# Grouped attention, new turn table: angles and weight splits move, two shifts per unit go to GpSimd, the maximum comes last in its turn

## The chip, the cores and the metric

The kernel runs on one core of a Trainium2 chip. The metric is the device time of one execution in microseconds. The core's engines have queues of their own and meet at semaphores: the tensor engine (PE; PEld is its weight load), the vector engine (DVE), the scalar engine (ACT), GpSimd (POOL) and SyncE (SP), which issues the large transfers.

## The reference

Four layers, each a cross-attention and a feed-forward part, on 4 x 256 tokens of width 256 with a context of 1601 rows. The change touches the attentions of layers 1 and 3, which have 16 query heads of width 128 over 4 key/value heads. Cut to what matters:

```python
# layer 3 (layer 1 has the same form, with x normalised first)
q = rms_norm((x @ Wq).reshape(B, S, 16, 128), q_norm_w)
k = rms_norm((ctx @ Wk).reshape(B, S_ctx, 4, 128), k_norm_w)
v = (ctx @ Wv).reshape(B, S_ctx, 4, 128)
probs = softmax(einsum("bqhd,bkhd->bhqk", q, repeat(k, 4)) * 128 ** -0.5)
out = einsum("bhqk,bkhd->bqhd", probs, repeat(v, 4)).reshape(B, S, 2048) @ Wo
# layer 1 only: the 256 tokens are keys too, and q and k are turned by position
emb = concat(pos * inv_freq, pos * inv_freq)          # 64 frequencies
x = x * cos(emb) + rotate_half(x) * sin(emb)
```

## The kernel before, in words

`run_layers` runs the stages one after another. `grouped_attention` is called twice: as `a1` with `rope=True` (layer 1, the rope stage) and as `a3` with `rope=False` (layer 3, the last attention stage). Each call has a first block (`plan_first`), which prepares the first group, and a main block with all the attention.

The main block works through 16 groups, a batch and a key/value head each. A group has two units of 512 query columns, and a unit one turn per tile of 128 keys: KT = 15 tiles in the rope stage (13 of context, 2 of tokens) and 13 in the last. So a group has 30 or 26 turns. In turn n the tensor engine makes `scores(n)` (L1184 to L1186) and `values(n - KT - 6)` (L1196). The scalar engine makes `exp(n - KT - 5)` (L1332) and `keep(n)`, a scaled copy of the scores into a ring (L1317). The vector engine makes `highest(n)`, the running maximum over a unit (L1551). The shift by the maximum, `shift(n - KT - 3)`, is made in the ring by the vector engine (L1568) or by GpSimd (L1438); `by_vector` says which, from the tile's number.

When a unit is through, MX transposes the running maximum on the tensor engine (L1152) and reduces it on the vector engine (L1559). NB broadcasts it on the tensor engine (L1163) and copies it on the scalar engine (L1326). MX0 and NB0 stand in turns 16 and 17 of a rope group (14 and 15 of the other), MX1 and NB1 in turns 1 and 2. In the vector engine's queue MX comes first in its turn, ahead of `highest` and `shift`. NB's matmuls wait for the reduce and, since they overwrite what the shifts read, for the vector engine's last shift of the unit before.

All other work is in a table written out by hand, `GROUP_TURNS`: a string for each turn, whose tasks prepare the next group. Every engine walks it in order. The names: KV, Q are products with their copies and squares (L1084, L1098; L1276, L1280, L1291; L1518, L1523); KN, QN norms; KR, QR rotation on GpSimd in two items each, products (L1393, L1394) and sums (L1400, L1401); KX, QX, OX transposes (L1113, L1122, L1130) with a high and a low part (L1489); Y the output product (L1141); N, NZ, NX the normalised tokens; PR, PX the positions; RA the angles on the vector engine and RS their sines on the scalar engine (L1339); GP, GA gathers from the stage before, in group 0 only (L1446, L1498). A `<` means the task of the group before. RA, RS and the other tasks of `NEXT_BATCH` are only done once per batch: the early ones in the third group of a batch, the `late` ones in the fourth, for the first three batches. The products and transposes share two banks of PSUM in turn.

W is the weights: W0 for K and V, W1 for Q, W2 for the output product. Each weight is used as a high and a low half. For the first groups (W0 and W1: groups 0 and 1; W2: groups 0 to 3) W splits them: SP loads them into the one buffer `wf`, the scalar engine copies the high half (L1260), the vector engine subtracts (L1476), and SP stores both halves and then issues the next load (L980). Later groups fetch the halves (L993). So SP's order is

```python
i = splits[("W", g, k)]
sp.wait_ge(w_lo, i)
store_weights(g, k)
if i < len(weights):
    load_weights(*weights[i][1:])
```

## Time and profile before

| | |
|---|---|
| median of 3 runs | 3602.94 us (3602.02 to 3603.24) |
| profiled execution, its own time | 3602.94 us |
| its span, first to last instruction | 3601.2 us |
| busy: PE, DVE, ACT, POOL | 3316.4, 2280.7, 2246.0, 1559.2 us |
| mean granted clock of the tensor engine | 0.959 |
| rope stage, main block | from 544 us to 1717 us |
| last attention stage, main block | from 2487 us to 3477 us |

A row of the profile names an engine, a line of the kernel, an operation and its tiles (output, then inputs, buffer numbers left out). A wait is idle time of an engine ahead of an instruction, put down to the instruction that released it. The granted clock is 1.00 at 2.4 GHz and 0.50 at 1.2 GHz; a stretch in between holds both.

### The profile page before, as it was taken

To read this page: it belongs to the slowest core of one execution; us is meant where nothing else is said; L and a number is where in the kernel's file an instruction comes from. 1 tells how busy PE (TensorE), PEld (TensorE's weight loads), DVE (VectorE), ACT (ScalarE), POOL (GpSimd) and SP (SyncE) were. 2 spreads that over 40 slices of the span, in tenths; PEclk is the share of its full clock that TensorE was granted. 3 is DMA by queue.
4 is the path that set the end of the run, shared out by engine and by line. 5 is a ranking of instruction groups with operands and counts; after the bars stand their busy time and mean duration, and the time that the engine had idled before them with its cause. 6 is when DMAs were issued, how large, how long until landed. Compare 5 with 4: busy or idle time off the path is not lost. (4 is left out here: it accounts for less than half of the span.)

```text
span 3601.2 us, 64159 instructions
## 1 busy us (share of the span) xinstructions
PE 3316.4 (92%) x23332; PEld 2857.9 (79%) x23332; DVE 2280.7 (63%) x4533; ACT 2246.0 (62%) x5204; POOL 1559.2 (43%) x1584
## 2 busy tenths in 40 slices
PE   6859958999999999999799999888999999999999
PEld 5658957888889888888666666577899999999888
DVE  8976746766676676666777777535655555555544
ACT  3326736777777767776376676515777777777743
POOL 0012146766667665763220220112565555555534
PEclk8879978999999999999899999989999999999999
DMA  5216522110120021000200000113221111120011
GB/s 189 92 40 218 216 89 85 68 61 30 48 79 30 30 84 42 31 19 24 92 19 38 1 38 1 75 39 115 71 84 48 54 73 42 43 84 31 30 39 39
DMA packets 74457, 227.83 MB, mean 63 GB/s; under 512 B 7780, under 2 KB 29472, under 8 KB 69152
## 3 DMA queue, kind: packets, MB, share of 16 engines
q1 hardware_dynamic: 68288, 184.34, 14.4%
q0 software_dynamic: 3696, 37.68, 2.8%
q8 instruction: 188, 3.08, 0.4%
q10 hardware_dynamic: 2160, 1.71, 0.2%
q14 instruction: 125, 1.02, 0.1%
HBM read 178.60 MB, written 45.11 MB: 62 GB/s over the span
## 5 line engine op out<-in xcount | busy, mean ns | idle before, releaser
L1551 DVE SCALAR_TENSOR_TENSOR a_peak<-ps,a_k_rstd,a_peak 128x512 f32<-128x512 f32 (+1 forms) x768 | 575.9, 750 | 617.6 <-ACT a_ring L1317 612.1
L1196 PE MATMUL ps<-a_v_rows,a_ring 128*128 128x129 f32 (+1 forms) x7168 | 934.8, 275 | 7.6 <-DVE a_o_rows L1577 3.8
L1317 ACT ACTIVATE a_ring<-ps,a_k_rstd 128x512 f32<-128x512 f32 (+1 forms) x896 | 615.5, 688 | 496.5 <-PE ps L1186 456.7
L1196 PEld LDWEIGHTS ps<-a_v_rows,a_ring 128*128 128x128 f32 (+1 forms) x7168 | 877.8, 191 | 26.0 <-ACT a_ring L1332 9.2
L1438 POOL TENSOR_TENSOR a_ring<-a_ring,a_negb 128x512 f32<-128x512 f32 (+1 forms) x506 | 645.7, 1297 | 246.0 <-ACT a_negb L1326 236.8
L1332 ACT ACTIVATE a_ring<-a_ring 128x512 f32<-128x512 f32 (+1 forms) x896 | 562.7, 631 | 18.6 <-DVE a_ring L1568 13.4
L1184 PE MATMUL ps<-a_qt,a_kt 128*128 128x512 f32 (+1 forms) x896 | 423.5, 473 | 5.0 <-PEq L73 5.0
L1084 PE MATMUL ps<-a_wr,a_ct 128*128 128x256 f32 (+1 forms) x2496 | 382.4, 291 | 36.8 <-DMA a_ct<-ctx_lo 15.9
L1084 PEld LDWEIGHTS ps<-a_wr,a_ct 128*128 128x128 f32 (+1 forms) x2496 | 346.6, 190 | 83.4 <-DVE a_k_rows L1518 25.6
L1186 PE MATMUL ps<-a_qt,a_kt 128*128 128x512 f32 (+1 forms) x896 | 356.6, 398 | 0.0
L1185 PE MATMUL ps<-a_qt,a_kt 128*128 128x512 f32 (+1 forms) x896 | 355.4, 397 | 0.0
L3407 ACT ACTIVATE a_probs<-ps 128x1024 f32<-128x1024 f32 x224 | 229.5, 1024 | 136.1 <-PE ps L3261 135.3
L1568 DVE TENSOR_TENSOR a_ring<-a_ring,ps 128x512 f32<-128x512 f32 x390 | 262.6, 676 | 2.8 <-ACT a_negb L1326 2.8
L3599 DVE TENSOR_REDUCE a_parts<-ps 128x1 f32<-128x448 f32 x384 | 222.1, 618 | 57.4 <-PE ps L3223 52.1
L1186 PEld LDWEIGHTS ps<-a_qt,a_kt 128*128 128x128 f32 (+1 forms) x896 | 166.8, 186 | 43.0
L1373 POOL TENSOR_SCALAR a_k_sq<-a_k_sq 128x4 f32<-128x4 f32 (+2 forms) x128 | 28.5, 223 | 368.7 <-ACT a_v_rows L1280 362.4
L1184 PEld LDWEIGHTS ps<-a_qt,a_kt 128*128 128x128 f32 (+1 forms) x896 | 169.9, 190 | 8.2 <-issue 5.6
L1185 PEld LDWEIGHTS ps<-a_qt,a_kt 128*128 128x128 f32 (+1 forms) x896 | 169.9, 190 | 2.5
L3261 PE MATMUL ps<-a_qt,a_kt 128*128 128x512 f32 x448 | 164.2, 448 | 2.5 <-ACT a_qt L3394 2.3
L1276 ACT ACTIVATE a_square<-ps 128x128 f32<-128x128 f32 (+1 forms) x448 | 124.6, 278 | 62.7 <-PE ps L1084 57.4
L1518 DVE TENSOR_TENSOR a_k_rows<-ps,a_kw 128x128 f32<-128x128 f32 (+1 forms) x448 | 126.2, 283 | 53.3 <-ACT a_v_rows L1280 53.2
L3223 PE MATMUL ps<-a_kt,a_qt 128*128 128x448 f32 (+1 forms) x512 | 154.3, 368 | 4.9 <-ACT a_kt L3375 1.2
(465 smaller groups left out, 6016.5 us busy)
## 6 DMA issues: line engine op xcount, KB each, us to landing
a_wr<-a_w SPq DMA_DIRECT2D x96, 512.0 KB, 4.5
a_w<-a_wr SPq DMA_DIRECT2D x32, 512.0 KB, 3.9
a_wr<-a_w SPq DMA_DIRECT2D x48, 256.0 KB, 3.5
a_ct<-ctx_hi SPq DMA_DIRECT2D x8, 1090.0 KB, 5.7
a_ct<-ctx_lo SPq DMA_DIRECT2D x8, 1090.0 KB, 7.9
f_we<-in_f_experts SPq DMA_DIRECT2D x8, 1088.0 KB, 8.5
...
```

The costliest lines, as they stand in the source:

```text
L1084: ins = pe.matmul(out[0:r, 0:2 * HD], src, wr[0][v][:, c * 2 * HD:(c + 1) * 2 * HD], start=(n == 0), stop=(n == 3 * DC - 1))
L1184: pe.matmul(out, kt[0][:, at:at + r], qt[0][:, cols], start=True, stop=False)
L1185: pe.matmul(out, kt[0][:, at:at + r], qt[1][:, cols], start=False, stop=False)
L1186: pe.matmul(out, kt[1][:, at:at + r], qt[0][:, cols], start=False, stop=True).then_inc(st_ready, 1)
L1196: ins = pe.matmul(m.ps[:, 6 + i // 2, (i % 2) * 256:(i % 2) * 256 + VW], slot(n)[0:r, i * P:(i + 1) * P], v_rows[u // NG % 2][0:r, t, :], ...
L1317: act.activation(slot(n)[0:r, :], m.ps[0:r, SCORE_BANKS[n % 3], :], ACT.Copy, scale=k_rstd[0:r, g % 2, t:t + 1]).then_inc(kept, 1)
L1332: act.activation(slot(n)[0:r, :], slot(n)[0:r, :], ACT.Exp).then_inc(exp_done, 1)
L1438: pool.tensor_tensor(slot(n)[0:r, :], slot(n)[0:r, :], negb[0:r, u % 2, :], ALU.add)\
L1551: dve.scalar_tensor_tensor(out=peak[0:r, :], in0=m.ps[0:r, SCORE_BANKS[n % 3], :], scalar=k_rstd[0:r, u // NG % 2, t:t + 1], in1=(slot(n - ...
L1568: dve.tensor_tensor(slot(n)[0:r, :], slot(n)[0:r, :], m.ps[0:r, MAX_BANK, :], ALU.add)\
L3407: act.activation(flat2(probs[n % 3][:, :, :]), flat2(m.ps[:, first:first + 2, :]), ACT.Exp)\
L3599: dve.tensor_reduce(to, slot(("R", h, j))[:, 0:n], AX.X, ALU.max, negate=True).then_inc(neg_done, 1)
```

## The change

`GROUP_TURNS` gets new tables. In the rope stage the angles go from RA0 to RA8 in one group, with RS in the next, to RA0 to RA2 in the third group of a batch and RA3 to RA9 and RS0 in the fourth; the query rotations QR move from turns 9 to 12 to turns 12 to 15, the key rotations KR0 to KR3 from 14, 15, 17, 18 to 16 to 19, KR4 and KR5 by two turns and one or two; KX1 goes from 22 to 23 and KX2 from 27 to 29; QN, N, NZ move by a few turns. W0 goes from turn 4 of the next group to turn 29 (25 in the other stage) of its own, right behind W2, which in the last stage goes from 25 to 24; W1 goes from 12 to 8.

The angles are computed into the tables themselves: the sine's and the cosine's argument each get a tensor, the cosine's by adding a quarter turn and taking a whole turn off where it is over half a turn, and RS makes both sines in place. That is 11 vector operations for 9. The wait for the last rotation of the batch before, which RS had, is now RA3's. `by_vector` gives the vector engine every second tile of the rope stage (7 of 15) where it had 9 of 15 (tiles 1, 2, 3, 5, 6, 7, 9, 10, 11). MX on the vector engine moves into the turn's task list, behind `outputs`, `highest` and `shift`.

```diff
--- before.py
+++ after.py
@@ -715,22 +715,22 @@
 
 GROUP_TURNS = {
     True: (
-        "QX1<", "MX1 KR6<", "NB1 KR7<", "Q0", "W0< PR0 GP4", "RS0 GP5", "Q1 GA4 GP6", "KX3< PX0 GA5 GP7 QN0",
-        "KV0 QN1 GA6 GP8", "OX0 KV1 QR0 RA0 GA7 GP9", "KV2 QR1 RA1 GA8 GP10", "KV3 QR2 RA2 GA9 GP11",
-        "KV4 KN0 QR3 W1 RA3 GA10 GP12", "KV5 RA4 GA11 GP13", "KV6 KR0 RA5 GA12 GP14", "KV7 KR1 RA6 GA13 GP15",
-        "MX0 KN1 GA14", "NB0 KV8 KR2 GA15", "QX0 KR3 RA7", "KV9 RA8", "KX0 KV10 N0", "KV11", "KX1 KN2 KV12",
-        "OX1 KR4 NZ0", "Y0 KR5", "KV13", "Y1", "KX2 KV14", "W2", "KN3 NX0",
+        "QX1<", "MX1 KR6<", "NB1 KR7<", "Q0 RA3", "RA4 PR0 GP4", "RA5 GP5", "Q1 RA6 GA4 GP6",
+        "KX3< RA7 PX0 GA5 GP7", "KV0 QN0 W1 RA8 GA6 GP8", "OX0 KV1 RA9 GA7 GP9", "KV2 QN1 RS0 RA0 GA8 GP10", "KV3 GA9 GP11",
+        "KV4 KN0 QR0 RA1 GA10 GP12", "KV5 QR1 GA11 GP13", "KV6 QR2 RA2 GA12 GP14", "KV7 QR3 GA13 GP15",
+        "MX0 KN1 KR0 GA14", "NB0 KV8 KR1 GA15", "QX0 KR2", "KV9 KR3", "KX0 KV10", "KV11 N0", "KV12",
+        "OX1 KX1 KN2", "Y0 NZ0", "KV13 KR4", "Y1 KR5", "KV14", "W2", "KX2 W0 KN3 NX0",
     ),
     False: (
-        "QX1<", "MX1", "NB1 KX2< KN3<", "Q0", "KX3< W0<", "", "Q1", "QN0", "OX0 KV0", "KV1 QN1", "KV2", "KV3 N0",
-        "KV4 KN0 W1", "KV5 QX0", "MX0 KV6 NZ0", "NB0", "KV7", "KX0 KV8", "KN1", "KV9", "KV10", "OX1 KX1", "Y0",
-        "KV11 KN2", "Y1", "KV12 W2 NX0",
+        "QX1<", "MX1", "NB1 KX2< KN3<", "Q0", "KX3<", "", "Q1", "QN0", "OX0 KV0 W1", "KV1 QN1", "KV2", "KV3 N0", "KV4 KN0",
+        "KV5 QX0", "MX0 KV6 NZ0", "NB0", "KV7", "KX0 KV8", "KN1", "KV9", "KV10", "OX1 KX1", "Y0",
+        "KV11 KN2", "Y1 W2", "KV12 W0 NX0",
     ),
 }
 
 FIRST_TASKS = {
     True: (
-        "GP0 V0 GP1 PR0 GP2 PX0 RA0 RA1 RA2 RA3 GA0 RA4 GA1 RA5 RA6 GA2 RA7 GP3 KV0 GA3 RA8 KV1 KV2 N0 KV3 "
+        "GP0 V0 GP1 PR0 GP2 PX0 RA0 RA1 RA2 RA3 GA0 RA4 GA1 RA5 RA6 GA2 RA7 GP3 KV0 GA3 RA8 RA9 KV1 KV2 N0 KV3 "
         "RS0 KN0 KV4 NZ0 KV5 V1 NX0 KR0 KV6 KV7 QN0 QN1 KR1 Q0 Q1 KX0 W1 KV8 KV9 KV10 KN1 QR0 QR1 KV11 KN2 QR2 "
         "KV12 KN3 QR3 KV13 KR2 KV14 KR3 QX0 KR4 KR5 KR6 KR7 KX1 KX2 KX3 QX1 W0"
     ),
@@ -757,7 +757,7 @@
     if kind in ("GP", "GA"):
         return g == 0
     if kind in NEXT_BATCH:
-        late = kind == "RS"
+        late = kind == "RS" or kind == "RA" and i >= 3
         return g % KVH == (KVH - 1 if late else KVH - 2) and g + KVH < GROUPS
     if kind in ("MX", "NB"):
         return g > 0 if i else g < GROUPS
@@ -873,7 +873,7 @@
             u, t = divmod(n, KT)
             if u == UNITS - 1:
                 return t % 3 > 0
-            return t % 4 > 0 and t < KT - 2 if rope else t % 4 == 3
+            return t % 2 == 1 if rope else t % 4 == 3
 
         by_turn = [by_vector(n) for n in range(TURNS)]
         shifts = {v: list(itertools.accumulate(int(b == v) for b in by_turn)) for v in (False, True)}
@@ -1332,11 +1332,9 @@
                         act.activation(slot(n)[0:r, :], slot(n)[0:r, :], ACT.Exp).then_inc(exp_done, 1)
 
                     def RS(g, _i):
-                        if attend:
-                            act.wait_ge(k_ready, rotated_k[("KR", g - 1, 2 * len(KB) - 1)])
-                        for i, (angle, table) in enumerate(((ang, cs[:, 1, :, :]), (tmp, cs[:, 0, :, :]))):
+                        for i in range(2):
                             act.wait_ge(angles, 2 * (turn_of_batch(g) - 1) + i + 1)
-                            act.activation(table, angle, ACT.Sin).then_inc(tab_ok, 1)
+                            act.activation(cs[:, i, :, :], cs[:, i, :, :], ACT.Sin).then_inc(tab_ok, 1)
 
                     def end_high(k):
                         act.wait_ge(end_turned, k + 1)
@@ -1595,14 +1593,15 @@
 
                     def RA(g, i):
 
+                        if i == 3 and attend:
+                            dve.wait_ge(k_ready, rotated_k[("KR", g - 1, 2 * len(KB) - 1)])
                         c1 = 6.28125
                         c2 = float(np.float32(0.0019353071795864769))
                         c3 = 2 * np.pi - c1 - c2
                         magic = 12582912.0
                         PI = 3.1415925
+                        cos, sin = cs[:, 0, :, :], cs[:, 1, :, :]
                         if i == 0:
-                            if turn_of_batch(g) > 1:
-                                dve.wait_ge(tab_ok, 2 * (turn_of_batch(g) - 1))
                             step(dve.tensor_tensor(ang, pos_f[:, :].unsqueeze(2).to_broadcast([P, KT, half]),
                                                    invf[:, :].unsqueeze(1).to_broadcast([P, KT, half]), ALU.mult))
                         if i == 1:
@@ -1610,16 +1609,17 @@
                         if i == 2:
                             step(dve.tensor_scalar(tmp, tmp, -magic, None, ALU.add))
                         if i in (3, 4, 5):
-                            step(dve.scalar_tensor_tensor(out=ang, in0=tmp, scalar=-(c1, c2, c3)[i - 3],
-                                                          in1=ang, op0=ALU.mult, op1=ALU.add))
+                            step(dve.scalar_tensor_tensor(out=sin, in0=tmp, scalar=-(c1, c2, c3)[i - 3],
+                                                          in1=ang if i == 3 else sin, op0=ALU.mult, op1=ALU.add))
                         if i == 6:
-                            dve.tensor_scalar(ang, ang, PI, -PI, ALU.min, ALU.max).then_inc(angles, 1)
+                            step(dve.tensor_scalar(cos, sin, np.pi / 2, None, ALU.add))
                         if i == 7:
-                            dve.wait_ge(angles, 2 * (turn_of_batch(g) - 1) + 1)
-                            step(dve.scalar_tensor_tensor(out=tmp, in0=ang, scalar=-1.0, in1=ang,
-                                                          op0=ALU.mult, op1=ALU.min))
+                            step(dve.tensor_scalar(tmp, cos, np.pi, -2 * np.pi, ALU.is_gt, ALU.mult))
                         if i == 8:
-                            dve.tensor_scalar(tmp, tmp, np.pi / 2, None, ALU.add).then_inc(angles, 1)
+                            step(dve.tensor_tensor(cos, cos, tmp, ALU.add))
+                        if i == 9:
+                            dve.tensor_scalar(cos, cos, PI, -PI, ALU.min, ALU.max).then_inc(angles, 1)
+                            dve.tensor_scalar(sin, sin, PI, -PI, ALU.min, ALU.max).then_inc(angles, 1)
 
                     def end_low(k):
                         dve.wait_ge(end_hi, k + 1)
@@ -1630,11 +1630,9 @@
                         dve.wait_ge(zeroed, ZEROED)
                         dve.wait_ge(norm_in, 16 * NORMS)
                     does = {"GA": GA, "PR": PR, "PX": PX, "RA": RA, "W": W, "N": N, "NZ": NZ, "NX": NX, "KV": KV, "Q": Q,
-                            "KX": KX, "QX": QX, "OX": OX, "Y": Y}
+                            "KX": KX, "QX": QX, "OX": OX, "Y": Y, "MX": MX}
                     for n, turn in enumerate(turns):
                         v, s = n - VALUE_LAG, n - SHIFT_LAG
-                        for _task, g, i in (task for task in turn if task[0] == "MX"):
-                            MX(g, i)
                         if attend and 0 < v < TURNS and v % KT == 0:
                             outputs(v // KT - 1)
                         if attend and n < TURNS and n % KT:
```

## Rows read from the trace of the kernel before

**Rows 1.** Windows: busy time (instructions) of PE, PEld, DVE, ACT, POOL; PEclk, DMA share, GB/s.

```profile
1201.97:1273.27 71.30, 70.10 (x506) 63.68 (x505) 44.35 (x79) 50.83 (x132) 46.66 (x50) 1.00 0.11 38
...
1273.27:1349.87 76.60, 71.65 (x511) 64.08 (x510) 57.81 (x98) 51.37 (x133) 53.51 (x51) 1.00 0.22 78
...
2858.50:2920.50 62.00, 61.47 (x449) 56.45 (x448) 35.71 (x70) 44.95 (x118) 33.79 (x35) 1.00 0.29 103
```

**Rows 2.** The tensor engine's waits, 544 to 1640: us in total, times, longest us.

```profile
PE ps L1084 <- DVE a_k_rows L1518: 15.5, 21, 2.0
...
PE ps L1141 <- DVE a_ot L1489: 11.5, 14, 0.8
...
PE ps L1163 <- DVE a_negmax L1559: 3.3, 4, 1.1
```

**Rows 3.** Order of time, all engines, one maximum of the rope stage: start, duration, instruction.

```profile
801.06 0.60 PE L1152 MATMUL ps<-ident,a_peak 128*128 128x128 f32 x4
...
801.26 0.69 ACT L1317 ACTIVATE a_ring<-ps,a_k_rstd 128x512 f32<-128x512 f32 x1 [0.54 <-PE ps L1186]
...
801.70 0.69 DVE L1559 TENSOR_REDUCE a_negmax<-ps 128x4 fp32r<-128x512 f32 x1 [1.17 <-PE ps L1152]
...
803.09 0.56 PE L1163 MATMUL ps<-ident_r,a_negmax 128*128 128x128 f32 x4
...
803.99 1.28 POOL L1438 TENSOR_TENSOR a_ring<-a_ring,a_negb 128x512 f32<-128x512 f32 x1
```

**Rows 4.** Order of time, two maxima of the last attention stage.

```profile
2873.29 0.60 PE L1152 MATMUL ps<-ident,a_peak 128*128 128x128 f32 x4
...
2876.05 0.60 PE L1163 MATMUL ps<-ident_r,a_negmax 128*128 128x128 f32 x4
...
2904.96 0.60 PE L1152 MATMUL ps<-ident,a_peak 128*128 128x128 f32 x4
...
2906.20 0.74 DVE L1551 SCALAR_TENSOR_TENSOR a_peak<-ps,a_k_rstd,a_ring 128x512 f32<-128x512 f32 x1
...
2906.86 0.67 DVE L1568 TENSOR_TENSOR a_ring<-a_ring,ps 128x512 f32<-128x512 f32 x1
...
2907.68 0.63 PE L1163 MATMUL ps<-ident_r,a_negmax 128*128 128x128 f32 x4 [0.53 <-DVE a_ring L1568]
```

**Rows 5.** Order of time, weight split in both grouped stages.

```profile
611.13 2.76 DVE L1476 TENSOR_TENSOR a_wr<-a_wf,a_wr 128x1024 fp32r<-128x1024 f32 x1
...
614.76 0.78 SPq L980 DMA_DIRECT2D a_wf<-in_a_wkv  x1
...
615.16 1.06 PE L1196 MATMUL ps<-a_v_rows,a_ring 128*128 128x129 f32 x8
...
2532.37 0.79 SPq L980 DMA_DIRECT2D a_wf<-in_a_wkv  x1
...
2532.46 1.06 PE L1196 MATMUL ps<-a_v_rows,a_ring 128*128 128x129 f32 x8
```

**Rows 6.** DMA issues, 540 to 720: size of each, us to landing.

```profile
a_wf<-in_a_wkv SPq DMA_DIRECT2D x2, 256.0 KB, 4.1
```

**Rows 7.** Windows, the first group's stalls, columns as in rows 1.

```profile
563.00:588.00 25.00, 16.26 (x59) 12.18 (x58) 15.55 (x23) 8.90 (x25) 22.57 (x25) 0.59 0.32 103
```

**Rows 8.** Order of time, vector engine, angles in the first block.

```profile
494.55 0.66 DVE L1616 TENSOR_SCALAR a_ang_tmp<-a_ang_tmp 128x960 f32<-128x960 f32 x1
495.52 1.15 DVE L1619 SCALAR_TENSOR_TENSOR a_ang_tmp<-a_ang_tmp 128x960 f32<-128x960 f32 x1
```

**Rows 9.** Order of time, tensor engine, turns 22 and 24 of a rope group.

```profile
815.57 0.91 PE L1084 MATMUL ps<-a_wr,a_ct 128*65 128x256 f32 x6 [0.35 <-DVE a_k_rows L1518]
...
821.82 1.66 PE L1141 MATMUL ps<-a_wr,a_ot 128*128 128x256 f32 x12 [0.81 <-DVE a_ot L1489]
```

**Rows 10.** Order of time, tensor engine, first group, and behind the sines.

```profile
578.99 1.12 PE L1152 MATMUL ps<-ident,a_peak 128*128 128x128 f32 x4 [2.62 <-DVE a_k_rows L1518]
...
1365.45 1.16 PE L1196 MATMUL ps<-a_v_rows,a_ring 128*128 128x129 f32 x8 [1.06 <-ACT a_ring L1332]
```

## The prediction

> **What bounds the kernel now.** I read the stretches first, one group of the two grouped-attention stages at a time [rows 1]. A steady group of the rope stage takes 71.30 us with the tensor engine busy for 70.10; a group of the last attention stage takes 62.00 us with 61.47 busy. Both run at the full clock (2.4 GHz). The vector engine is busy for 44.35 of 71.30 us, GpSimd for 46.66. So the tensor engine sets the pace, and an edit elsewhere counts only as far as it makes or ends an idle moment there. Next, who the tensor engine waits for [rows 2]: almost only the vector engine, 15.5 + 11.5 + 3.3 = 30.3 us on the three rows shown. With the idle time of the angle groups (below) that is the most that relief of the vector engine can give. Then the order of events around one maximum, in each stage [rows 3, 4], the weight split [rows 5, 6], and the irregular groups [rows 7 to 10].
>
> The sum is made against the profiled execution: 3602.94 us, span 3601.2 us, and 3602.94 is also the median of the runs.
>
> **1. Maximum after the running maximum and a shift.** In the rope stage, counted from the end of the peak transposes (801.06 + 0.60 = 801.66), the vector engine's reduce runs from 0.04 to 0.73 and the broadcast matmuls (L1163) start at 1.43, right behind the tensor engine's own work [rows 3]: no wait. In the new order three operations come first to last. `highest` must wait for the scalar engine's copy, which ends at 801.95, 0.29 after the transposes. It starts at about 0.33. The steps from start to start are 0.66 us for `highest` (2906.20 to 2906.86) [rows 4] and about 0.60 us for a shift whose duration is 0.67 [rows 4], since neighbours overlap a little (the reduce, of 0.69, is followed after 0.61 too). That a shift stands in this turn is the other edit's doing: the turn is the second of a unit, 18 turns of lag make its shift that of tile 13, and the new rule `t % 2 == 1` gives 13 to the vector engine, where before it was GpSimd's. So the reduce starts at 1.59, ends at 2.28, and L1163 starts at about 2.33 instead of 1.43: 0.90 us. This happens once in each of 30 units (not in unit 0, where the shift does not exist yet, nor in the last, where no `highest` stands before it); in three of them L1163 already waits about as long for the vector engine, as part of the 3.3 us row [rows 2]. 27 x 0.90 = **+24.3 us**. Below, the bound is 0, if the vector engine got ahead; above, 30 x 0.99 (with no overlap between the operations) = 30.
>
> In the last stage the shift of tile 11 already stands in this turn and L1163 already waits for it: it starts at 2907.68, 2.12 after the transposes end at 2905.56 [rows 4]. The three operations only change order, and the chain now starts at the copy instead of the transposes: 2.33 against 2.12, +0.20. In the other unit of a group a K/V product stands between, and L1163 starts 2.16 after the transposes (2873.29 + 0.60 to 2876.05) without a wait: +0.17. 15 x 0.20 + 15 x 0.17 = **+5.6 us**.
>
> **2. W0 right behind W2.** For the first two groups of each stage W is no fetch but a split: load into the one buffer `a_wf`, copy by the scalar engine, subtraction by the vector engine. The load for W0 is issued only after W2's subtraction, and takes 4.1 us to land [rows 5, 6]. In the rope stage the subtraction ends at 613.89 and the load is issued at 614.76, so it lands at 618.9. Before, W0 stood six turns behind W2, 14 us at 71.30 / 30 = 2.38 us a turn, later than that. Now the scalar engine reaches W0 one turn behind W2, at about 612.5, and waits there, with the exponentials and the copies of two later turns queued behind it. SP's store and next load move with it and delay nobody. The subtraction starts about 0.3 us sooner, because its turn loses a shift, and may be less stretched by GpSimd, so I take landing at 618.2. The copy (0.62) and an exponential (0.63) come next: the value matmuls due at 615.16 start at 619.4, +4.2 us. The maximum two operations later is late too (0.6 of copy, 0.6 exponential, 0.7 keep, then 2.0 of vector work, against 1.8 us of tensor work): 2.0 more beyond edit 1. 6.2 us, twice: **+12.4**. In the last stage the load goes out at 2532.37 [rows 5] and W2 is itself one of the shorter turns earlier, so about 2530.2; landed 2534.3, copied and one exponential done 2535.5, against values due at 2532.46: 3.1 us, and 1.9 more at the maximum, which waits 0.53 already. At the second instance W2 has to wait for Y1 in its own turn first, but comes earlier against the tensor engine by 0.8 us: 5.0 + 4.2 = **+9.2 us**. Bounds: 0, and 8 us each (32), the wait of the scalar engine from 612.5 to the copy's end plus the maximum.
>
> Such a stall also lowers the clock. From 563 to 588 the tensor engine stood still for 8.7 of 25 us, 2.62 at the longest, and the granted clock fell to 0.59, a mixture of 1.2 and 2.4 GHz [rows 7, 10]. I estimate two thirds of a turn's 2.38 us (71.30 / 30) lost per stall, 1.6 x 4 = **+6.4 us**; bounds 0 and the 10 us (0.41 x 25) that the stretch shows, for two of them.
>
> By the Trainium skill (DMA: Bandwidth & Descriptors, anatomy of one DMA) a transfer of the software path costs about 2.0 us and its bytes over 436 GB/s, 2.6 us for 256 KB; this load goes the hardware path, behind two stores of 512 KB, and its row says 4.1, so the trace does not agree. With 2.6 the four stalls would be 1.5 us shorter each and the forecast 6 us lower.
>
> **3. Angles.** The first block gets 11 angle operations instead of 9. It loses one of 1.15 us and one of 0.66 and gains one two-input operation (1.15) and three of 0.66 [rows 8], before the sines, on which scalar engine and GpSimd wait: +1.3, with the issue **+1.4 us**. In the three later batches the additions don't matter; what counts is where they stand. The group with the angle chain took 76.60 us against 71.30, of which 71.65 and 70.10 are work: 4.95 idle against 1.20 [rows 1]. Spread over two groups with one a turn, alongside fewer shifts, I give back 2.3 of these 3.75: 3 x 2.3 = **-7 us** (0 to -11). The sines keep their four scalar-engine items (two table loads and two sines) and move from turn 5 to turn 10; their stall stays near the 1.06 seen [rows 10], at nothing net (a fuller turn could make it 2 us more per batch). The new wait of the angles for the last rotation ends during turn 3, which has 1.4 us of Q product on the tensor engine as cover; without the cover the vector engine's queue would lose about 1 us, three times.
>
> **4. The other moves.** Tensor idle before Y0 is 0.81 us in 15 groups, because the low part of OX1 comes behind a shift that stays [rows 9]. KX1's transposes (0.44 us of issue) now stand between: 15 x 0.45 = **-6.7**. In turn 22 a K/V product waits 0.35 us for a bank behind KX1 [rows 9]; with KX1 gone, 14 x 0.36 = **-5.0**. In group 0 the vector engine stands for gathers and the tensor engine behind it, 2.62 us at the longest [rows 10]. GpSimd issues these gathers between rotations; with the rotations two or three turns later, KR0 and KR1 (two products of 1.28 [rows 3] and two sums of half the size) come behind the last gather, which goes out about 4 us earlier, and the vector engine finds several others ready: **-5** (0 to -12, if the clock stays up too). The shifts themselves: two per unit go from 0.67 us on the vector engine to 1.28 on GpSimd [rows 3, 4], 46.66 + 4 x 1.28 = 51.8 of 71.30 us there; hidden. W1 at turn 8 and the fetches are ready sooner: nothing.
>
> **Sum.** 24.3 + 5.6 + 12.4 + 9.2 + 6.4 + 1.4 = 59.3; less 7 + 6.7 + 5.0 + 5 = 23.7; net +35.6, so 3638.5 us, 1.0% slower.
>
> **The rivals.**
> *The load is hidden* (the change of place does nothing there): the scalar engine's queue is deep enough, or the load lands before 612.5. Against it: the single buffer and 4.1 us. Price: 28 us less, 3610.5.
> *GpSimd becomes the bound.* Rotations, queries and now eight shifts per unit crowd into turns 12 to 19. It decides if a shift ends later than its exponential is due, two turns or 4.8 us on. Price: two of the four added shifts in each of 15 groups, 2.56 x 15 = +38, 3677. Against it: 73% busy.
> *The vector engine gets ahead* (faster). In turns 1 and 16 everything is done before the transposes end, and each wait on the vector engine goes. It decides at a reduce that ends less than 1.4 us after the transposes. Price: edit 1 costs nothing (-29.9), and the relief gives the waits of rows 2 in full and 11 us of the angle groups, 41 instead of 23.7 (-17.6): 3591. Against it: the scalar engine's copy ends 0.29 after the transposes, and three operations don't fit in the 1.1 us from there.
> *The clock* stays low for the whole of 10 us after each stall: 3638.5 + 4 x 8.4 = 3672.
>
> **How the numbers follow.** Forecast 0.67, load hidden 0.08, GpSimd 0.08, vector ahead 0.06, clock 0.11. Range 3608 to 3674: it takes in the hidden load and the low clock and leaves out the faster case and the GpSimd case. A measurement here tells 0.2% (7 us) from no change. Faster 0.06 (the vector case); within 0.2% 0.04 (the forecast with its gains at their bounds and half the stall); slower 0.90.
>
> **What would show it.** Right: L1163 waiting 0.9 us behind the vector engine in both halves of a rope group, the reduce starting behind an L1568; the scalar engine idle 5 us and more before an L1260 at the end of groups 0 and 1, and the clock below 1.00 there; steady rope groups of about 72 us (71.30 + 1.8 - 0.8). Wrong: L1163 starting 1.43 after the transposes as before; an idle GpSimd-to-scalar wait at L1332 in each group; the W0 copy without a wait.

## The result, and the profile of the changed kernel

The changed kernel takes 3654.1 us, the median of runs from 3651.8 to 3655.6, against 3602.9 before: a ratio of 1.0142, 95% interval 1.0118 to 1.0165. It is 51 us slower. Its profiled execution took 3653.4 us with a span of 3651.7, 50.5 us more than the 3601.2 before. By the starts of the score matmuls (L1184) these 50.5 us lie as follows: the first block -0.8, the rope stage +26.1, the stretch between the stages +0.6, the last attention stage +22.6, what follows it +2.0. One execution of one experiment below ran at a granted clock of 0.735 and took 4186 us; its number leaves that one out.

Windows of the changed kernel, one for each group, columns as in [rows 1]: in the rope stage the second group, in which the tensor engine stands for a weight split, a steady group, a third group and a fourth group of a batch; then such a split group and a steady one of the last stage.

```profile
607.32:687.09 79.77, 74.24 (x506) 66.78 (x505) 45.50 (x79) 53.17 (x136) 53.63 (x54) 0.94 0.15 50
...
1218.76:1290.51 71.75, 69.89 (x506) 63.57 (x505) 42.02 (x76) 51.16 (x132) 51.71 (x54) 1.00 0.11 38
1290.51:1364.86 74.35, 71.26 (x511) 64.22 (x510) 49.09 (x89) 51.51 (x133) 53.62 (x55) 1.00 0.23 80
1364.86:1444.46 79.60, 71.85 (x506) 63.45 (x505) 49.84 (x84) 54.62 (x136) 51.89 (x54) 1.00 0.10 34
...
2555.86:2627.48 71.62, 65.34 (x448) 59.37 (x447) 39.27 (x66) 47.38 (x123) 36.88 (x34) 0.93 0.16 56
...
2821.24:2883.64 62.40, 61.67 (x448) 56.33 (x447) 33.75 (x62) 44.91 (x118) 33.52 (x34) 1.00 0.12 43
```

Against [rows 1] a steady rope group is only 0.5 us longer, and a steady group of the last stage 0.4. GpSimd has gone from 46.66 to 51.71 us, as forecast (51.8). The third group is 2.3 us shorter than before. The long ones are the split groups and the fourth, in which most of the angles and the sines now stand: 80.7, 79.6 and 79.6 us in the first three batches, where the old kernel had 74.9, 73.7 and 73.7.

The tensor engine's waits in the changed kernel, 544 to 1640, as in [rows 2]:

```profile
PE ps L1163 <- DVE a_negmax L1557: 26.1, 29, 4.3
PE ps L1196 <- ACT a_ring L1332: 10.9, 5, 3.7
PE ps L1084 <- DVE a_k_rows L1516: 10.8, 12, 2.6
PE ps L1141 <- DVE a_ot L1487: 5.0, 13, 0.4
PE ps L1113 <- POOLq L1400: 4.4, 4, 1.2
```

The three rows of before shrank and swapped: Y's wait (L1141) from 11.5 to 5.0, the K/V products' (L1084) from 15.5 to 10.8, and the maximum's (L1163) grew from 3.3 to 26.1. Two rows are new: values that wait for an exponential (L1196; two behind the weight splits, three behind the sines), and key transposes (L1113) that wait for GpSimd, one in the first group and three in the fourth ones.

In order of time, one maximum of the changed rope stage, to be laid beside [rows 3]:

```profile
1221.57 0.60 PE L1152 MATMUL ps<-ident,a_peak 128*128 128x128 f32 x4
...
1222.48 0.75 DVE L1549 SCALAR_TENSOR_TENSOR a_peak<-ps,a_k_rstd,a_ring 128x512 f32<-128x512 f32 x1 [0.80 <-ACT a_ring L1317]
...
1223.15 0.68 DVE L1566 TENSOR_TENSOR a_ring<-a_ring,ps 128x512 f32<-128x512 f32 x1
...
1223.75 0.68 DVE L1557 TENSOR_REDUCE a_negmax<-ps 128x4 fp32r<-128x512 f32 x1
...
1224.49 0.66 PE L1163 MATMUL ps<-ident_r,a_negmax 128*128 128x128 f32 x4 [0.73 <-DVE a_negmax L1557]
```

From the end of the transposes (1222.17) the running maximum starts at 0.31, the reduce at 1.58, the broadcast at 2.32. The forecast had 0.33, 1.59 and 2.33. What it left out: behind a wait L1163 takes 0.66 us and not 0.56, so a unit loses 0.89 + 0.10 = 0.99 us, not 0.90.

In order of time, W0's load, copy and the stalled values, at the end of the rope stage's first group and of the last stage's:

```profile
609.03 0.79 SPq L980 DMA_DIRECT2D a_wf<-in_a_wkv  x1
...
613.17 0.63 ACT L1260 ACTIVATE a_wr<-a_wf 128x512 fp32r<-128x512 f32 x1 [5.27 <-DMA a_wf<-in_a_wkv]
...
614.37 2.09 PE L1196 MATMUL ps<-a_v_rows,a_ring 128*128 128x129 f32 x8 [3.64 <-ACT a_ring L1332]
...
2557.75 0.79 SPq L980 DMA_DIRECT2D a_wf<-in_a_wkv  x1
...
2563.57 0.63 ACT L1260 ACTIVATE a_wr<-a_wf 128x512 fp32r<-128x512 f32 x1 [7.45 <-DMA a_wf<-in_a_wkv]
...
2564.77 2.09 PE L1196 MATMUL ps<-a_v_rows,a_ring 128*128 128x129 f32 x8 [5.50 <-ACT a_ring L1332]
```

The scalar engine stands for 5.27 and 7.45 us, with the exponentials behind it. Eight value matmuls that took 1.06 us in [rows 5] then take 2.09: the clock is at 1.2 GHz.

Last, the fourth group of the changed kernel in order of time: an angle operation and the values of turn 7, two angle operations beside GpSimd's work, the table load and the sines, and who comes late behind them.

```profile
1380.94 1.15 DVE L1612 SCALAR_TENSOR_TENSOR a_cs<-a_ang_tmp,a_cs 128x960 f32<-128x960 f32 x1
...
1382.34 0.69 DVE L1575 TENSOR_TENSOR a_o_rows<-ps,a_rsum 128x512 f32<-128x512 f32 x1
...
1383.17 2.02 PE L1196 MATMUL ps<-a_v_rows,a_ring 128*128 128x129 f32 x16 [1.21 <-DVE a_o_rows L1575]
...
1386.55 1.55 DVE L1617 TENSOR_SCALAR a_ang_tmp<-a_cs 128x960 f32<-128x960 f32 x1
...
1389.60 1.65 DVE L1619 TENSOR_TENSOR a_cs<-a_cs,a_ang_tmp 128x960 f32<-128x960 f32 x1
...
1394.26 1.28 ACT L1337 ACT_TABLE_LOAD   x1
...
1395.55 1.90 ACT L1337 ACTIVATE a_cs<-a_cs 128x960 f32<-128x960 f32 x2
...
1397.47 1.28 ACT L1332 ACT_TABLE_LOAD   x1
...
1399.45 1.16 PE L1196 MATMUL ps<-a_v_rows,a_ring 128*128 128x129 f32 x8 [1.16 <-ACT a_ring L1332]
...
1400.48 0.19 POOL L1371 TENSOR_SCALAR a_k_sq<-a_k_sq 128x4 f32<-128x4 f32 x1 [10.25 <-ACT a_v_rows L1280]
```

In turn 7 the vector engine copies the unit's output behind an angle operation, and the values of the next unit wait 1.21 us for that. The sines and two table loads hold the scalar engine from 1394.26 to 1398.75, 4.5 us. The values of turn 12 wait 1.16 us, and GpSimd, which has been idle for 10.25 us, starts the key norm late. Its rotations and the key transposes of turn 20 are pushed back by that.

### The profile page after: what moved, and what is told of

It reads as the page before. It is cut to its first block and busy times, and to the rows that moved or that the text cites. A ratio compares the mean times of both kernels' runs of the same rounds, so it can differ in the third digit from the quotient of the medians.

```text
span 3651.7 us, 64134 instructions
## 1 busy us (share of the span) xinstructions
PE 3330.9 (91%) x23332; PEld 2863.2 (78%) x23332; DVE 2248.3 (62%) x4479; ACT 2251.3 (62%) x5204; POOL 1628.3 (45%) x1646
## 5 line engine op out<-in xcount | busy, mean ns | idle before, releaser
L1196 PE MATMUL ps<-a_v_rows,a_ring 128*128 128x129 f32 (+1 forms) x7168 | 940.4, 276 | 25.7 <-ACT a_ring L1332 19.4
L1196 PEld LDWEIGHTS ps<-a_v_rows,a_ring 128*128 128x128 f32 (+1 forms) x7168 | 881.5, 192 | 44.4 <-ACT a_ring L1332 28.1
L1436 POOL TENSOR_TENSOR a_ring<-a_ring,a_negb 128x512 f32<-128x512 f32 (+1 forms) x568 | 723.2, 1294 | 307.8 <-ACT a_negb L1326 296.7
L1332 ACT ACTIVATE a_ring<-a_ring 128x512 f32<-128x512 f32 (+1 forms) x896 | 562.8, 631 | 64.8 <-POOL a_ring L1436 57.4
L1184 PE MATMUL ps<-a_qt,a_kt 128*128 128x512 f32 (+1 forms) x896 | 424.5, 474 | 5.0 <-PEq L73 5.0
L1084 PE MATMUL ps<-a_wr,a_ct 128*128 128x256 f32 (+1 forms) x2496 | 377.8, 289 | 32.2 <-DMA a_ct<-ctx_lo 16.7
L1084 PEld LDWEIGHTS ps<-a_wr,a_ct 128*128 128x128 f32 (+1 forms) x2496 | 345.7, 188 | 73.0 <-issue 17.1
L1566 DVE TENSOR_TENSOR a_ring<-a_ring,ps 128x512 f32<-128x512 f32 x328 | 220.8, 677 | 2.8 <-ACT a_negb L1326 2.8
L1184 PEld LDWEIGHTS ps<-a_qt,a_kt 128*128 128x128 f32 (+1 forms) x896 | 170.4, 190 | 8.2 <-issue 5.6
```

The source lines that it names most:

```text
L1084: ins = pe.matmul(out[0:r, 0:2 * HD], src, wr[0][v][:, c * 2 * HD:(c + 1) * 2 * HD], start=(n == 0), stop=(n == 3 * DC - 1))
L1184: pe.matmul(out, kt[0][:, at:at + r], qt[0][:, cols], start=True, stop=False)
L1196: ins = pe.matmul(m.ps[:, 6 + i // 2, (i % 2) * 256:(i % 2) * 256 + VW], slot(n)[0:r, i * P:(i + 1) * P], v_rows[u // NG % 2][0:r, t, :], ...
L1332: act.activation(slot(n)[0:r, :], slot(n)[0:r, :], ACT.Exp).then_inc(exp_done, 1)
L1436: pool.tensor_tensor(slot(n)[0:r, :], slot(n)[0:r, :], negb[0:r, u % 2, :], ALU.add)\
L1566: dve.tensor_tensor(slot(n)[0:r, :], slot(n)[0:r, :], m.ps[0:r, MAX_BANK, :], ALU.add)\
```

## The experiments

Each was run beside the kernel before; "against before" is the difference of the medians of executions taken together, and the changed kernel stands at +51.2.

### Taking single parts of the change out again

**The reduce first again**, in the changed kernel:

```diff
-                            "KX": KX, "QX": QX, "OX": OX, "Y": Y, "MX": MX}
+                            "KX": KX, "QX": QX, "OX": OX, "Y": Y}
...
                         v, s = n - VALUE_LAG, n - SHIFT_LAG
+                        for _task, g, i in (task for task in turn if task[0] == "MX"):
+                            MX(g, i)
```

> The new kernel with one thing undone: the maximum's reduce stands first in its turn on the vector engine again. The shift of tile 13 stays on the vector engine. My theory: the broadcast matmuls (L1163) wait for two things, the reduce and the vector engine's last shift of the unit, and both stand in this turn. So only the start of the chain moves, from the scalar engine's copy (0.33 us after the peak transposes) back to the transposes (0.04, but three operations in a row all the same): about 0.2 us per unit in 30 units of each grouped stage, 6 us and 5.6 us, together -11 us or so, 3642. Rival (the order alone is what costs): L1163 is back at 1.43 us after the transposes, -24 us in the rope stage and -6 in the last, 3624.

Measured: 3647.4 us, +43.8 against before (ratio 1.0120, 1.0105 to 1.0136). L1163 starts 0.20 us sooner and each unit of both stages is 0.22 us shorter at that place; a last-stage group takes 62.0 us instead of 62.45, a steady rope group 71.5, since turn 21 gives 0.22 back; by the starts of the scores the two stages are 5.4 and 7.8 us shorter (the medians differ by 7). The rival is out: the order alone is worth little, since L1163 also waits for the shift of tile 13, which stands in the same turn.

**Tile 13 to GpSimd again**:

```diff
-            return t % 2 == 1 if rope else t % 4 == 3
+            return t % 2 == 1 and t < KT - 2 if rope else t % 4 == 3
```

> The new kernel with one thing undone: the shift of tile 13 goes to GpSimd again, the order of the turn stays new (running maximum, then reduce). My theory: L1163 starts behind running maximum and reduce, 0.33 + 0.66 + 0.69 + 0.05 = 1.7 us after the transposes instead of 2.3, and the tensor engine's own work covers 1.4 of it: 0.6 us saved in 27 to 30 units, -16 to -18 us, 3637; the last attention stage is untouched. Rival (GpSimd is near its limit, so a fifth long shift in half the turns costs there): 30 more shifts of 1.28 us on GpSimd delay exponentials, and the time rises or stays within 5 us.

Measured: 3672.3 us, +68.7 against before (1.0181, 1.0168 to 1.0195), so 18 us slower than the changed kernel where I expected 17 faster. My theory of the place was right and that of the sum wrong. Its waits of the tensor engine, 544 to 1640, the scalar engine's wait for GpSimd in turn 19, and the window of a steady group:

```profile
PE ps L1113 <- POOLq L1400: 19.3, 15, 2.9
PE ps L1084 <- DVE a_k_rows L1516: 16.3, 19, 2.6
...
PE ps L1163 <- DVE a_negmax L1557: 4.5, 3, 4.2
...
1286.82 0.63 ACT L1332 ACTIVATE a_ring<-a_ring 128x512 f32<-128x512 f32 x1 [2.13 <-POOL a_ring L1436]
...
1241.00:1313.48 72.48, 70.59 (x507) 63.55 (x505) 40.76 (x74) 50.91 (x132) 54.17 (x57) 1.00 0.10 38
```

L1163's wait went from 26.1 to 4.5 us: 0.6 us per unit, as expected. But turn 20 became 1.65 us and turn 21 0.20 us longer in each steady group. There the key transposes (L1113) and the K/V products now wait. In turn 19 the scalar engine waits 2.13 us for GpSimd's shift of tile 14, where it waits 0.23 in the changed kernel. GpSimd is busy for 54.17 of 72.48 us, 75%, and still late at that place. A steady group loses 0.7 us and the angle groups more; by the starts of the scores the rope stage is 21.5 us longer than in the changed kernel.

**The old shift rule**, which gives GpSimd tile 13 too (tile 14 it has in both), but takes tiles 2, 6 and 10 from it:

```diff
-            return t % 2 == 1 if rope else t % 4 == 3
+            return t % 4 > 0 and t < KT - 2 if rope else t % 4 == 3
```

> The new kernel with the old rule of who shifts in the rope stage (GpSimd the first tile of each four and tiles 13 and 14, the vector engine the other nine). Against the run in which only tile 13 went to GpSimd, GpSimd has here three shifts less per unit. My theory after that run (GpSimd's rotations gate the key transposes of turn 20, and one long shift more makes them late by more than the maximum saves): here the 0.6 us per unit are saved at L1163 as there, and the key transposes no longer wait, so 30 x 0.6 = -18 us, 3636; the vector engine has two shifts more, which may cost some of it in the angle groups. Rival (the order of the vector engine's turn at tile 13, not GpSimd, makes turn 20 late): the key transposes still wait 0.5 us and more per group and it stays at 3665 to 3675.

Measured: 3660.3 us, +58.9 against before (1.0167, 1.0153 to 1.0181). I expected 3636. A steady group takes 72.1 us; L1163's wait is down to 0.14 us, and K/V products of turns 20 and 21 wait 0.16 and 0.64 us. In turn 19 of the same group:

```profile
1269.48 0.63 ACT L1332 ACTIVATE a_ring<-a_ring 128x512 f32<-128x512 f32 x1 [0.87 <-POOL a_ring L1436]
```

So less work on GpSimd in sum doesn't help. What this kernel has in common with the last is tile 13 on GpSimd, in the turns of the rotations: its shift of tile 14 comes behind that and the products of a rotation, and the scalar engine waits for it. The vector engine has two shifts more per unit here, and no run separates what they add.

**W0 back in turn 4**, in both stages:

```diff
-        "QX1<", "MX1 KR6<", "NB1 KR7<", "Q0 RA3", "RA4 PR0 GP4", "RA5 GP5", "Q1 RA6 GA4 GP6",
+        "QX1<", "MX1 KR6<", "NB1 KR7<", "Q0 RA3", "W0< RA4 PR0 GP4", "RA5 GP5", "Q1 RA6 GA4 GP6",
...
-        "OX1 KX1 KN2", "Y0 NZ0", "KV13 KR4", "Y1 KR5", "KV14", "W2", "KX2 W0 KN3 NX0",
+        "OX1 KX1 KN2", "Y0 NZ0", "KV13 KR4", "Y1 KR5", "KV14", "W2", "KX2 KN3 NX0",
```

> The new kernel with W0 back in the fifth turn of the next group, in both stages (W1 and W2 stay where the change has them). My theory: the four stalls of groups 1 and 2 of each stage go with the low clock behind them; by the two traces the groups were longer by 8.0 + 7.4 us and 9.6 + 6.3 us than their neighbours' change explains, some 29 us in all: 3625. Rival 1 (the wait goes but the clock falls anyway for other reasons, W2's own load): about 6 us less of it, 3631. Rival 2 (the load is late wherever W0 stands, it only stalls another turn): within 5 us of 3654.

Measured: 3623.1 us, +19.6 against before (1.0052, 1.0038 to 1.0065): 31 us of the 51. Windows of its split groups:

```profile
610.54:682.35 71.81, 69.97 (x506) 63.42 (x505) 45.16 (x79) 53.07 (x136) 53.66 (x54) 1.00 0.16 56
...
2544.29:2606.75 62.46, 61.73 (x449) 56.38 (x447) 39.13 (x66) 47.33 (x124) 36.91 (x34) 1.00 0.19 65
```

Against the changed kernel's 79.77 and 71.62 us these groups lose 7.96 and 9.16 us. The windows split that: idle time of the tensor engine falls from 79.77 - 74.24 = 5.53 to 1.84 us, and its busy time from 74.24 to 69.97 at a clock of 1.00. Over all four split groups it is 17.4 us of idle and 13.0 us of work at the lower clock.

**A second staging buffer** in the last stage alone, with W0 left behind W2, and its load issued a split ahead:

```diff
-        wf = st.sb("wf", [P, max(WIDTHS)])
+        wf = [st.sb(f"wf{i}", [P, max(WIDTHS)]) for i in range(1 if rope else 2)]
...
+            def ahead(j):
+                return int(attend and not rope and 0 < j < len(weights) and weights[j][2] != weights[j - 1][2])
...
-                        if i < len(weights):
-                            load_weights(*weights[i][1:])
+                        for j in (i, i + 1):
+                            if j < len(weights) and j - ahead(j) == i:
+                                load_weights(*weights[j][1:])
```

> The new kernel with a second staging buffer for the weight split in the last attention stage alone (the rope stage has no room for one), so that W0's load is issued a split ahead, when W1's split is done; W0 stays right behind W2. My theory (the stall is the wait for a load that can only be issued after W2's subtraction): the last stage's groups 1 and 2 come from 71.6 and 68.8 us to about 62.5 to 63, -15 us, with the low clock of the stretch gone too: 3639; the rope stage's two stalls stay. Rival (it is the two copies and two subtractions in neighbouring turns that crowd the engines, not the load): these groups stay at 67 or above, -4 us at most.

Measured: 3637.2 us, +33.4 against before (1.0092, 1.0077 to 1.0107). Windows of the two split groups of its last stage:

```profile
2557.70:2620.20 62.50, 61.77 (x447) 56.43 (x447) 39.39 (x66) 47.40 (x124) 37.42 (x35) 1.00 0.18 64
2620.20:2683.10 62.90, 62.17 (x451) 56.81 (x450) 37.98 (x72) 46.84 (x121) 36.19 (x35) 1.00 0.20 68
```

71.6 and 68.8 us became 62.5 and 62.9, with W0 where the change put it. So it is the load behind the one buffer, and neither the place nor the crowded turns by themselves.

**The old angles and sines**: nine operations in turns 9 to 19 of the third group, the sines in turn 5 of the fourth (the code of the old kernel's RA and RS, and its table with them):

```diff
...
-        "KX3< RA7 PX0 GA5 GP7", "KV0 QN0 W1 RA8 GA6 GP8", "OX0 KV1 RA9 GA7 GP9", "KV2 QN1 RS0 RA0 GA8 GP10", "KV3 GA9 GP11",
+        "KX3< PX0 GA5 GP7", "KV0 QN0 W1 GA6 GP8", "OX0 KV1 RA0 GA7 GP9", "KV2 QN1 RA1 GA8 GP10", "KV3 RA2 GA9 GP11",
...
```

> The new kernel with the angle chain and the sines of the old kernel, in code and in place (nine operations in turns 9 to 19 of a batch's third group, sines in turn 5 of the fourth), everything else new. My theory: what the change lost in the fourth group (79.6 us now, 73.7 before, three times: 17.7 us) comes back and what it won in the third (74.3 against 76.6, three times: 7 us) is lost again, net -11 us, 3643; the first block has one operation pair fewer, -1. Rival (the fourth group is long because of the shifts given to GpSimd and the later rotations, not because of the angles): it stays near 79, and the third grows by 2.3: +7 us, 3661.

Measured: 3647.8 us, +44.2 against before (1.0117, 1.0102 to 1.0133), 7 us faster than the changed kernel. The fourth group takes 75.0 us, but the third 77.7, more than the 76.6 of before: L1163 waits 2.12 us there in turn 17, with RA6 in the turn ahead of the maximum's. So the old places are only 1.2 us per batch better than the new ones, and both are worse than in the old layout. Turn 0 of the fourth group keeps the 0.5 us that it has over a steady one in the changed kernel, so these are not the angles': KX2 and the normalised tokens (NX0) stand together in the turn ahead.

**Copies instead of sines** in the three later batches, so that the kernel leaves their sines out:

```diff
-                            act.activation(cs[:, i, :, :], cs[:, i, :, :], ACT.Sin).then_inc(tab_ok, 1)
+                            act.activation(cs[:, i, :, :], cs[:, i, :, :], ACT.Copy if attend else ACT.Sin).then_inc(tab_ok, 1)
```

> The new kernel with the two sines of each later batch replaced by plain copies of the same size (the sines of batches 2 to 4 are left out, and so are the table loads that stand around them). A batch's fourth group takes 79.6 us now, 7.8 over a steady one. My theory before this run: the sine and its two table loads on the scalar engine are some 3 to 4 us of the 7.8 (the waits in turns 12, 20 and part of turn 9 follow them), the seven angle operations and the pushed-back outputs the rest: about 76 us, three times, -11 us, 3643. Rival 1 (all of it is the vector engine's angle operations): 79, -2 us. Rival 2 (all of it is the sines): 73, -20 us, 3634.

Measured: 3646.0 us, +42.2 against before (1.0114, 1.0099 to 1.0130). The window of a fourth group of it, which lasts 76.75 us against 79.60:

```profile
1363.71:1440.46 76.75, 71.32 (x506) 63.46 (x505) 49.84 (x84) 52.59 (x134) 51.88 (x54) 1.00 0.10 35
```

Turn 12 is 1.42 us shorter and turn 20 1.37: together the 2.8 us that the sines with their table loads cost. The other 5.0 us over a steady group stay, 1.45 in turn 7, 1.37 in turn 9, 0.65 in turn 10, 1.0 in turns 20 and 21 and 0.5 in turn 0. All but the last I read as the angle operations; no run takes these out alone.

### Single parts of the change in the old kernel

**The reduce behind**, alone (the first experiment the other way round):

```diff
-                            "KX": KX, "QX": QX, "OX": OX, "Y": Y}
+                            "KX": KX, "QX": QX, "OX": OX, "Y": Y, "MX": MX}
...
-                        for _task, g, i in (task for task in turn if task[0] == "MX"):
-                            MX(g, i)
```

> The old kernel with one part of the change: the maximum's reduce behind the running maximum and the shift of its turn. Tile 13's shift stays on GpSimd. My theory: in the rope stage L1163 starts 1.7 us after the transposes against 1.43 of the tensor engine's own work, 0.3 us in about 27 units, +8; in the last stage 0.2 us in 30 units, +6: 3617. Rival (the vector engine's queue behind the reduce gains what the reduce loses, so the move is neutral): within 4 us of 3603.

Measured: 3625.2 us, +23.8 (1.0066, 1.0053 to 1.0079), more than I expected. One of its maxima in order of time:

```profile
1209.77 0.60 PE L1152 MATMUL ps<-ident,a_peak 128*128 128x128 f32 x4
...
1212.09 0.66 PE L1163 MATMUL ps<-ident_r,a_negmax 128*128 128x128 f32 x4
```

L1163 starts 1.72 us after the transposes against 1.43, as expected, and takes 0.66 instead of 0.56: 0.39 per unit, 0.76 in a steady group, 11.6 us in 30 units, where I had 8. The rope stage is 15.5 us longer in all; the other 4 us lie in its first five groups, and I can't say what they are. The last stage's units add 0.22 each, 6.6 in all.

**The new shift rule**, alone:

```diff
-            return t % 4 > 0 and t < KT - 2 if rope else t % 4 == 3
+            return t % 2 == 1 if rope else t % 4 == 3
```

> The old kernel with one part of the change: the new rule of who shifts in the rope stage (odd tiles the vector engine, even tiles GpSimd). My theory: L1163 now waits for the shift of tile 13 behind reduce and running maximum, 2.0 us after the transposes against 1.43: +0.6 us in 27 to 30 units, +17; the vector engine has two operations less per unit, which takes up to 6 us off the waits of the angle groups: 3602 + 11 to 17, about 3616. Rival (the relief is worth more than the new wait, since GpSimd no longer has tiles 13 and 14 in a row ahead of the last exponentials): 3602 or below.

Measured: 3625.1 us, +21.3 (1.0049, 1.0036 to 1.0063). Its waits, 544 to 1640:

```profile
PE ps L1163 <- DVE a_ring L1568: 18.4, 28, 1.7
```

The new wait costs 0.77 us per unit, a little more than the 0.6 expected. The relief that I counted on is small: 0.26 and 0.29 us in turns 10 and 21 of a steady group, while the third groups take 78.6 us, 2 more than before. By the starts of the scores the rope stage is 16.4 us longer, inside what I expected; 5.1 us more lie between the stages, where the edit changes nothing.

**W0 behind W2**, with W2 a turn earlier in the last stage, alone:

```diff
-        "QX1<", "MX1 KR6<", "NB1 KR7<", "Q0", "W0< PR0 GP4", "RS0 GP5", "Q1 GA4 GP6", "KX3< PX0 GA5 GP7 QN0",
+        "QX1<", "MX1 KR6<", "NB1 KR7<", "Q0", "PR0 GP4", "RS0 GP5", "Q1 GA4 GP6", "KX3< PX0 GA5 GP7 QN0",
...
-        "OX1 KR4 NZ0", "Y0 KR5", "KV13", "Y1", "KX2 KV14", "W2", "KN3 NX0",
+        "OX1 KR4 NZ0", "Y0 KR5", "KV13", "Y1", "KX2 KV14", "W2", "W0 KN3 NX0",
```

> The old kernel with one part of the change: W0 right behind W2 in both grouped stages (and W2 one turn earlier in the last, as in the change). My theory: the same stalls as in the new kernel, +31 us by the run that took them out of it: 3634. Rival (the stall is long only because the new layout brings the scalar engine there earlier, with KX2 before W0): under +20 us, below 3623.

Measured: 3629.7 us, +28.3 (1.0082, 1.0067 to 1.0097). The four groups are 7.0, 6.8, 9.4 and 5.5 us longer. The stall belongs to this edit and needs no other.

**The later places of rotations, KX1 and W1**, with everything else as before (the task strings of the changed kernel, W0 and the angles in their old turns):

```diff
...
-        "KV4 KN0 QR3 W1 RA3 GA10 GP12", "KV5 RA4 GA11 GP13", "KV6 KR0 RA5 GA12 GP14", "KV7 KR1 RA6 GA13 GP15",
+        "KV4 KN0 QR0 RA3 GA10 GP12", "KV5 QR1 RA4 GA11 GP13", "KV6 QR2 RA5 GA12 GP14", "KV7 QR3 RA6 GA13 GP15",
-        "MX0 KN1 GA14", "NB0 KV8 KR2 GA15", "QX0 KR3 RA7", "KV9 RA8", "KX0 KV10 N0", "KV11", "KX1 KN2 KV12",
+        "MX0 KN1 KR0 GA14", "NB0 KV8 KR1 GA15", "QX0 KR2 RA7", "KV9 KR3 RA8", "KX0 KV10", "KV11 N0", "KV12",
-        "OX1 KR4 NZ0", "Y0 KR5", "KV13", "Y1", "KX2 KV14", "W2", "KN3 NX0",
+        "OX1 KX1 KN2", "Y0 NZ0", "KV13 KR4", "Y1 KR5", "KV14", "W2", "KX2 KN3 NX0",
```

> A version that keeps of the change only the later places of the rotations, queries, KX1 and W1 (and W2's in the last stage), and has the old shift rule, the old order of the maximum, W0 in its old place and the old angles and sines. My theory: the old time less what the change won: 14 to 15 times 0.44 at Y0, 14 times 0.36 in turn 22, 3 us in group 0: 3602.9 - 14.7 = 3588, 0.4% faster than before. Rival (the wins came from the relief of the vector engine, not from the places): within 4 us of 3603.

Measured: 3614.8 us, +13.4 (1.0034, 1.0021 to 1.0046): slower, where I expected 0.4% faster. In order of time, turns 19 and 20 of a steady group of it:

```profile
1474.36 1.30 POOL L1438 TENSOR_TENSOR a_ring<-a_ring,a_negb 128x512 f32<-128x512 f32 x1
...
1475.69 0.63 ACT L1332 ACTIVATE a_ring<-a_ring 128x512 f32<-128x512 f32 x1 [1.30 <-POOL a_ring L1438]
...
1476.79 0.27 ACT L1276 ACTIVATE a_square<-ps 128x128 f32<-128x128 f32 x1
...
1478.53 0.97 PE L1084 MATMUL ps<-a_wr,a_ct 128*128 128x256 f32 x6 [0.56 <-DVE a_k_rows L1518]
```

GpSimd's shift (of tile 14, next after its shift of tile 13) stands behind a rotation's products. The scalar engine waits 1.30 us for it before its exponential; the squares of the K/V item stand behind that in its queue; the item's bank comes free late, and the next K/V product waits 0.56 us. The two turns are 0.83 and 0.62 us longer, which eats the gain at Y0 and in turn 22. So the later rotations need the new shift rule, and that rule costs 0.6 us at each maximum: in the change one pays for the other.

**KX1 one turn later**, alone:

```diff
-        "MX0 KN1 GA14", "NB0 KV8 KR2 GA15", "QX0 KR3 RA7", "KV9 RA8", "KX0 KV10 N0", "KV11", "KX1 KN2 KV12",
-        "OX1 KR4 NZ0", "Y0 KR5", "KV13", "Y1", "KX2 KV14", "W2", "KN3 NX0",
+        "MX0 KN1 GA14", "NB0 KV8 KR2 GA15", "QX0 KR3 RA7", "KV9 RA8", "KX0 KV10 N0", "KV11", "KN2 KV12",
+        "OX1 KX1 KR4 NZ0", "Y0 KR5", "KV13", "Y1", "KX2 KV14", "W2", "KN3 NX0",
```

> The old kernel with one place changed in the rope stage: KX1 stands one turn later, behind OX1, and nothing else. My theory: it takes 0.44 us off the wait before Y0 and 0.36 off the K/V product of turn 22, with the overlap that each wait costs 0.5 to 1.3 us per group, in 14 groups: -7 to -18 us, 3590. Against the version that moved the rotations too (it had new waits of 0.55 and 0.64 us in turns 20 and 21, behind a late shift on GpSimd) these waits are absent, since GpSimd's tasks are where they were. Rival (one of them comes back in a turn close behind): within 4 us of 3602.

Measured: 3587.0 us, -16.8 against before (0.9951, 0.9937 to 0.9964): faster than both kernels, with one task moved by one turn. A steady group's window, and the Y0 of the same kernel (compare [rows 1, 9]):

```profile
1188.86:1259.11 70.25, 69.85 (x506) 63.62 (x505) 44.19 (x79) 50.69 (x133) 46.66 (x50) 1.00 0.11 39
...
1463.16 1.66 PE L1141 MATMUL ps<-a_wr,a_ot 128*128 128x256 f32 x12 [0.39 <-DVE a_ot L1489]
```

The tensor engine's idle time in a group fell from 1.20 to 0.40 us, and the wait of 0.35 us in turn 22 is gone. Turns 22 to 24 change by -1.01, +0.44 and -0.45, so 1.0 us for each group.

## Why the forecast held, and where it didn't

The sum was +35.6 us, the measurement +51.2, inside the range and with the sign given. Step by step:

**Step 1, the maximum: right, slightly small.** 0.99 us per unit instead of 0.90, since the broadcast after a wait lasts 0.10 longer; 27 x 0.99 = 26.7 against 24.3. In the last stage 0.22 and 0.22 against 0.20 and 0.17: 6.6 against 5.6. What it had named as the other edit's doing holds too: the two parts alone cost 0.39 and 0.77 per unit, and the reduce taken back alone returned 0.22.

**Step 2, W0: the mechanism right, its two terms mis-sized against each other.** I gave 12.4 + 9.2 = 21.6 us to the stalls and 6.4 to the clock. The windows say 17.4 and 13.0. The values stalled for 3.64 us where I had 4.2, and the maximum behind them for 0.77 where I had 2.0, in the changed kernel's first split group; the clock cost 3.3 us for each stall instead of 1.6. In the last stage the load needed 5.82 us from its issue to the copy (2557.75 to 2563.57), not the 4.1 of the rope stage. The sum, 30.4, is near the 28.0. The load issued ahead shows that it is the buffer.

By the Trainium skill (DMA: Bandwidth & Descriptors, anatomy of one DMA), a transfer of the software path of this size would take about 2.6 us, an estimate from its figures. These two loads are issued by SyncE, each behind two stores of the same queue, and took 4.1 and 5.8; they are not transfers of that path, so the trace neither bears the figure out nor refutes it.

**Step 3, the angles: this step failed.** It read "alongside fewer shifts, I give back 2.3 of these 3.75: 3 x 2.3 = -7 us" and the sines' move "at nothing net (a fuller turn could make it 2 us more per batch)". The third group did get 2.3 us shorter. But the fourth got 5.9 us longer, 5.4 more than a steady one. It is now 7.8 us over a steady group. Of these 2.8 are the sines with their table loads, in a turn where values and the key norm hang on the scalar engine (shown by the copies in their place). The old kernel's fourth group, where by the task table only the sines stand, was 2.4 us over a steady one, so "at nothing net" was nearly right for the sines: 0.5 us per batch. The rest, 5.0 us, is in turns 0, 7, 9, 10, 20 and 21, where the products and values wait for the vector engine and GpSimd. That these are the angle operations is the reading of the rows, not shown by a run of its own, and the 0.5 in turn 0 is something else. The third group is 2.8 us better than a steady one (-2.3 against +0.5), but 0.99 of that is its second maximum, whose wait it had before already. So the move of the angles and sines costs 3 x (5.4 - 1.8) = +10.8 us where I had -7: 18 us, more than the miss of the whole sum. My error was to count idle time that could be given back, and not to ask what the second half of the chain would delay where it is put.

**Step 4, the other moves: small terms too low.** Y0's wait fell to 0.38 us and the one of turn 22 went, together 1.0 us per group instead of 0.45 + 0.36; 15 x 1.0 = 15.0 against 11.7. The relief of the vector engine, which I had put at nothing, gives 0.27 and 0.19 us in turns 10 and 21 of a steady group, 6.9 us in 15 (the old shift rule gives the 0.27 back). The first group gained 3.2 us net, where I had 5, but not by the path that I gave. Its windows, before and changed:

```profile
544.22:611.35 67.13, 56.02 (x288) 46.08 (x289) 42.90 (x71) 40.07 (x109) 47.44 (x50) 0.80 0.24 79
...
543.40:607.32 63.92, 51.54 (x288) 43.15 (x289) 38.98 (x67) 40.00 (x109) 52.08 (x54) 0.90 0.24 83
```

The tensor engine's idle time did not fall (11.1 and 12.4 us); its busy time did, by 4.5 us, at a granted clock of 0.90 instead of 0.80. The first block was 0.8 us sooner and not 1.4 later. In the profiles of the six kernels with the old first block the attention starts between 540.8 and 544.9 us, and in those with the new one between 541.4 and 548.4, so one profile can't tell a difference of this size.

With these numbers the terms give 26.7 + 6.6 + 30.4 + 10.8 - 0.8 - 15.0 - 6.9 - 3.2 + 0.6 (between the stages) + 2.0 (the end) = 51.2; the spans differ by 50.5. It is a rough account, as the first group's 3.2 holds a little of other terms. That the forecast came as near as 15.6 us is in part luck: the costs of steps 1 to 3 were 24 us too low, 18 of them in step 3, and the gains of step 4, 8 us too low, took a third of that back.

**The rivals.** The hidden load is out (the scalar engine waits 5.27 us). The vector engine ahead is out (L1163 waits in every unit). GpSimd as the bound: not in the changed kernel's steady groups, but one shift away. A sign that I had named for being wrong did appear: the scalar engine waits for GpSimd's shifts at L1332 52 times between 544 and 1640 (55.5 us in all, 4.4 before). In a steady group the tensor engine doesn't wait behind it, so the sign was badly chosen. With tile 13 back on it, GpSimd decides a turn in every group, at 75% busy; my argument "73% busy" against this rival was no argument. The low clock: it did stay at 1.2 GHz for 6.8 to 10.2 us at each stall, near the rival's 10, but that cost 2.5 to 4.3 us a stall (3.3 in the mean), where I had 1.6 and the rival 10. The rival's price was wrong: the engine at half its clock does half the work, so a stretch of 10 us loses 5 us at most. Executions of one experiment's kernel differ by up to 12 us, so differences below that rest on the groups of the traces; steady groups of one trace repeat to 0.1 us.
